# Staging eleven weight units ahead of a mixture layer, and moving its first groups' steps, in a four-layer kernel

## The chip, the cores and the metric

One NeuronCore of a Trainium2 chip. The metric is the device time of one execution of the whole program in microseconds (us); less is better. TensorE is PE in the rows (its weight loads are PEld), VectorE is DVE, ScalarE is ACT, GpSimd is POOL, and SyncE's queue, which issues most transfers, is SP.

## What is computed

2,048 tokens (16 sequences of 128) of width 256, in float32. Four residual layers follow one another:

```python
x = x + xattn0(ctx, ctx, layernorm(x))      # long convolution of key-value products
x = x + ffn0(layernorm(x))                  # 16 experts, top 4 in 2 of 4 groups, plus a shared expert
x = x + xattn1(layernorm(x), ctx, ctx)      # q.T k softmaxed over features, times v
x = x + ffn1(layernorm(x))                  # below
```

The last layer is the one that the change is about:

```python
probs = softmax(x @ Wg.T); rw, sel = top_k(probs, 2); rw = rw / rw.sum(-1)
base1, base3 = x @ W1.T, x @ W3.T           # W1, W3: (896, 256)
for k in range(2):
    x1 = base1 + lora1[sel[k]](x)           # A1: (8, 32, 256), B1: (8, 896, 32)
    x3 = base3 + lora3[sel[k]](x)
    x2 = silu(x1) * x3
    out += (x2 @ W2.T + lora2[sel[k]](x2)) * rw[k]
```

## The kernel before

The program has three blocks after one another: the first layer (to about 122 us of the span), the second layer (`moe_phase`, to about 299 us), and `tail_phase`, which does the third and the fourth layer together (299 to 789 us). Every engine's order is written by hand, as Python loops; an engine takes its instructions in that order and waits on semaphores.

**The routed loop of the second layer** (174 to 285 us) goes through 40 pairs of 128-row tiles. GpSimd gathers the rows of a tile by an indirect DMA (L1033) into a ring of eight tiles; TensorE turns them (L857), multiplies them with the expert's weights (L873, L896); ScalarE copies the result to `y_out` (L973), and SP stores it, 256 KB for a pair, into `slots_scratch` (L769). In front of the stores of pairs 0 to 3 SP issues one load of 384 KB each (L768): units 0 to 3 of the last layer's weights, into `lora_stage_early`.

**The last layer's weights** are eight chunks of 128 x 1536, cut into 16 units of 128 x 768. Units 0 and 1 are the chunk with A1, A3 and B2, units 2n+2 and 2n+3 are chunk n of the 896 hidden features. A float32 product is made of three products of a high and a low part, so each unit is split: ScalarE rounds it to `lora_w_hi` (`high_weights`, L1618), VectorE takes the difference to `lora_w_lo` (`low_weights`, L1819). The ring has four slots: unit k is loaded when unit k - 4 has been split.

**Groups and steps.** `tail_phase` takes the 16 token tiles in eight groups of two. Steps S run from -7 to 59; g = S // 7, n = S % 7. Step S of 0 to 55 is chunk n of group g. At the same time group G = g + 1 goes through the third layer and the router: `scores` at n = 0, `exponentials` and `attention_out` at n = 1, `turn` at n = 2, `logits` at n = 3, the ratio's exponential at n = 4, `spread_picks` at n = 5, `picks_copies` and `low_rank_in` at n = 6. So steps -7 to -1 are group 0's own attention, with no chunks beside them.

**A chunk's chain.** TensorE makes `base(F)` (L1442, x with W1 and W3), adds the low-rank part of the first pick `low_rank(F, 0)`, and one step later of the second, `low_rank(F, 1)` (both L1457). Behind each ScalarE makes the silu (L1625) and VectorE the product (L1953). GpSimd then weights the second pick (L1748, `weight`) and adds both (L1753, `both`), ScalarE rounds the two (L1631, L1635, `hidden_high`), VectorE makes the low parts (L1959, `hidden_low`), and two steps after `base` TensorE makes `down` and `terms` (L1489, L1502). `base(F)` waits until the products of chunk F - 2 are done, and in group 0 until chunk n is split:

```python
if g == 0:
    pe.wait_ge(lo_split, 2 * (n + 2))
if F >= 2:
    pe.wait_ge(prod_done, 2 * (F - 1))
```

The inputs of `low_rank` are the router's masks times the product with A1 and A3: `picks_copies` (ScalarE, L1678, L1682), `inputs_product` (VectorE, L1942), `inputs_high` (ScalarE, L1642, `am_hi`), and the low parts `am_lo` on GpSimd (L1759) and VectorE (L1948). GpSimd also gathers the second layer's rows of later token tiles (`gathers`, L1728), which VectorE adds to x (`add_routed`, L1829 to L1844). Group 0's wait for GpSimd's reciprocal root (L1768) stands before `normalize` (L1852). `find_inverse` and `scale_context` (L1862, L1870) make what `attention_out` (L1538) needs beside the exponentials (L1657). ScalarE's exp and silu lie in different tables, and an `ACT_TABLE_LOAD` stands where it changes; `warm` (L1684) is a one-column exponential that loads the first.

## Time and profile before

| | before |
|---|---|
| median of 3 runs | 794.3 us (794.25 to 794.47) |
| profiled execution, its own time | 791.16 us |
| its span | 789.4 us |
| TensorE busy | 713.2 us (90%), 4849 matmuls |
| VectorE busy | 507.8 us (64%) |
| GpSimd busy | 384.9 us (49%) |
| ScalarE busy | 340.5 us (43%) |
| mean granted TensorE clock | 0.959 |

The span is counted from the first instruction to the last, and the profiled execution's own time is 1.8 us more than it. A row of the timeline gives the start, the duration, the engine, the line, what is written and read and how often, and in brackets how long the engine had been idle before it and what released it.

### The profile page before, as it was taken

The numbers are of one execution on the slowest core, as the hardware profiler recorded it, in microseconds if no ns is written. First come the engines' busy times: TensorE is split into PE (matmuls) and PEld (weight loads), VectorE is DVE, ScalarE is ACT, GpSimd is POOL, SyncE is SP. The second block draws the span as 40 slices with busy tenths as digits, with TensorE's granted clock in tenths as the row PEclk, the third lists the DMA queues.
The fourth block names the chain that finished last, engine by engine and source line by source line (L and its number), as shares of the span: only waits on it lengthen the run. The fifth ranks groups of instructions, "written<-read, shape, count | busy, mean of one in ns | idle before, by whom it ended". The sixth has DMA issues, their size and how long they took to land.

```text
span 789.4 us, 13948 instructions
## 1 busy us (share of the span) xinstructions
PE 713.2 (90%) x4849; PEld 635.7 (81%) x4849; DVE 507.8 (64%) x1296; ACT 340.5 (43%) x698; POOL 384.9 (49%) x450
## 2 busy tenths in 40 slices
PE   4899988959999991778999999999999999999995
PEld 2444557848999980668899999999999999999995
DVE  3999997975666645676566566575574675653422
ACT  2563633245666652265444253444434533443221
POOL 5876956047766605544264363543652643322322
PEclk9999998988999995679999999999999999999999
DMA  8675505946866764424021020010020110000000
GB/s 246 196 166 133 142 27 125 210 108 179 245 195 197 163 146 126 155 71 130 1 61 34 8 61 28 14 59 22 29 63 5 41 41 1 2 15 1 14 1 14
DMA packets 44595, 68.61 MB, mean 87 GB/s; under 512 B 7376, under 2 KB 32240, under 8 KB 44528
## 3 DMA queue, kind: packets, MB, share of 16 engines
q0 software_dynamic: 10080, 28.72, 16.5%
q1 hardware_dynamic: 34352, 38.97, 15.5%
q8 instruction: 41, 0.67, 0.4%
q14 instruction: 26, 0.21, 0.1%
q10 hardware_dynamic: 96, 0.04, 0.0%
HBM read 50.77 MB, written 14.84 MB: 83 GB/s over the span
## 4 chain that ended last, share of the span: by engine, by line
PE 53%; POOL 3%; DVE 2%; ACT 2%; issue 2%; POOLq 0%; DVEq 0%
PE psum L1457 20%; PE psum L1442 10%; PE psum L1489 9%; PE psum L1502 4%; PE psum L1475 3%; PE psum L1538 2%; PE psum L1515 2%; PE psum L1528 2%; POOL rows_back L1728 1%; PE psum L1556 1%; ACT lora_w_hi L1618 1%; DVE lora_w_lo L1819 0%; PE psum L1546 0%; PE psum L1569 0%; PE psum L1576 0%
## 5 line engine op out<-in xcount | busy, mean ns | idle before, releaser
L1953 DVE TENSOR_TENSOR hid<-hid,psum 128x256 f32<-128x256 f32 x112 | 47.0, 420 | 152.2 <-ACT hid L1625 152.2
L1457 PE MATMUL psum<-am_hi,lora_w_hi 128*128 128x256 f32 x448 | 127.4, 284 | 2.0 <-DVE am_lo L1948 2.0
L1748 POOL TENSOR_TENSOR hid<-hid,ratio_sb 128x256 f32<-128x256 f32 x56 | 41.5, 741 | 176.9 <-DVE hid L1953 176.7
L1457 PE MATMUL psum<-am_hi,lora_w_lo 128*128 128x256 f32 x448 | 127.4, 284 | 0.0
L1457 PE MATMUL psum<-am_lo,lora_w_hi 128*128 128x256 f32 x448 | 127.2, 284 | 0.0
L1625 ACT ACTIVATE hid<-psum 128x256 f32<-128x256 f32 x112 | 42.9, 384 | 183.3 <-PE psum L1457 183.2
L1033 POOL DMA_INDIRECT rows_in<-y_scratch,slot_token x80 | 76.0, 950 | 30.9 <-issue 26.5
L1457 PEld LDWEIGHTS psum<-am_hi,lora_w_hi 128*128 128x128 f32 x448 | 86.2, 192 | 2.2 <-POOL am_lo L1759 2.1
L1457 PEld LDWEIGHTS psum<-am_hi,lora_w_lo 128*128 128x128 f32 x448 | 86.3, 193 | 0.0
L1457 PEld LDWEIGHTS psum<-am_lo,lora_w_hi 128*128 128x128 f32 x448 | 86.2, 192 | 0.0
L1728 POOL DMA_INDIRECT rows_back<-slots_scratch,comb_idx x64 | 66.8, 1043 | 39.2 <-POOLq L697 23.7
L1442 PE MATMUL psum<-lora_x_hi,lora_w_hi 128*128 128x256 f32 x224 | 67.8, 302 | 3.5 <-DVE lora_w_lo L1819 3.5
L1959 DVE TENSOR_TENSOR hid_lo<-hid,hid_hi 128x256 fp32r<-128x256 f32 x112 | 56.8, 528 | 13.1 <-ACT hid_hi L1631 8.0
L1442 PE MATMUL psum<-lora_x_lo,lora_w_hi 128*128 128x256 f32 x224 | 63.1, 282 | 0.0
L327 POOL TENSOR_TENSOR kv<-ctx_t 128x1024 f32<-128x1024 f32 (+2 forms) x48 | 57.4, 1284 | 11.6 <-PE psum L448 11.6
L1442 PE MATMUL psum<-lora_x_hi,lora_w_lo 128*128 128x256 f32 x224 | 62.9, 281 | 0.0
L873 PE MATMUL psum<-moe_w_hi,moe_xt_hi 128*128 x160 | 49.2, 307 | 0.0
L591 DVE TENSOR_TENSOR prod<-psum,q_t 128x1024 f32<-128x1024 f32 (+1 forms) x64 | 41.2, 685 | 8.4 <-PE psum L448 6.2
L1442 PEld LDWEIGHTS psum<-lora_x_hi,lora_w_hi 128*128 128x128 f32 x224 | 42.7, 191 | 4.6 <-DVE lora_w_lo L1819 4.2
L873 PE MATMUL psum<-moe_w_lo,moe_xt_hi 128*128 x160 | 45.9, 287 | 0.0
L1489 PE MATMUL psum<-hid_hi,lora_w_hi 128*128 128x512 f32 x112 | 44.6, 398 | 1.3 <-DVE hid_lo L1959 1.3
L873 PE MATMUL psum<-moe_w_hi,moe_xt_lo 128*128 x160 | 45.4, 284 | 0.0
(250 smaller groups left out, 2050.2 us busy)
## 6 DMA issues: line engine op xcount, KB each, us to landing
slots_scratch<-y_out SPq DMA_DIRECT2D x40, 256.0 KB, 3.3
stage<-in_moe_weights SPq DMA_DIRECT2D x18, 384.0 KB, 3.8
moe_w_lo<-in_moe_weights POOLq DMA_DIRECT2D x18, 384.0 KB, 7.1
lora_stage_early<-in_lora_weights SPq DMA_DIRECT2D x16, 384.0 KB, 3.5
x_sb<-in_x SPq DMA_DIRECT2D x4, 512.0 KB, 6.3
ctx_t<-in_ctx_t SPq DMA_DIRECT2D x4, 512.0 KB, 7.3
y_scratch<-y SPq DMA_DIRECT2D x8, 256.0 KB, 2.2
x_sb<-shared_out POOLq DMA_DIRECT2D x4, 512.0 KB, 5.3
```

Source lines behind the costliest of these rows:

```text
L327: last = nc.gpsimd.tensor_tensor(kv[:, n % KV_SLOTS, :, first:first + shape[2] * shape[3]].rearrange("p n (i j) -> p n i j", j=shape[3]), ...
L591: last = nc.vector.tensor_tensor(prod[:, :, j, i], y_ji, query[:, :, i].unsqueeze(2).broadcast_to(shape), ALU.mult)
L873: last = nc.tensor.matmul(gu_banks[q % 2][:, k * DIM:(k + 1) * DIM], xp, wp, start=(c == 0 and j == 0), stop=(c == HALVES - 1 and j == 2))
L1033: nc.gpsimd.indirect_dma_start(out=rows_in[:, i % ROW_SLOTS, :], out_offset=None, in_=y_dram[:, :], in_offset=bass.IndirectOffsetOnAxis(ap ...
L1442: nc.tensor.matmul(x_banks[F % 2][:, w * GT:(w + 1) * GT], wp, xp, start=(w == 0 and c == 0 and k == 0), stop=False, skip_group_check=True)
L1457: last = nc.tensor.matmul(x_banks[F % 2][:, w * GT:(w + 1) * GT], wp, ap, start=False, stop=(half == 1 and k == 2), skip_group_check=True)
L1489: last = nc.tensor.matmul(term_banks[half][:, :], wp, hp, start=(n == 0 and j == 0), stop=(n == FB - 1 and j == 2))
L1625: nc.scalar.activation(f[:, F % 2, k, :], x_banks[F % 2][:, 0:GT], ACT.Silu).then_inc(silu_done, 1)
L1728: nc.gpsimd.indirect_dma_start(out=rows_back[:, t % ROW_TILES, k * DIM:(k + 1) * DIM], out_offset=None, in_=slots_dram[:, :], in_offset=ba ...
L1748: nc.gpsimd.tensor_tensor(f[:, F % 2, 1, :], f[:, F % 2, 1, :], ratio_sb[:, F // FB % 2, :], ALU.mult)\
L1953: nc.vector.tensor_tensor(f[:, F % 2, k, :], f[:, F % 2, k, :], x_banks[F % 2][:, GT:2 * GT], ALU.mult)\
L1959: nc.vector.tensor_tensor(hid_lo[:, F % 2, which, :], f[:, F % 2, which, :], hid_hi[:, F % 2, which, :].bitcast(FP32), ALU.subtract).then_ ...
```

## The change

Eleven units instead of four are loaded in the routed loop (one in front of each of the stores of pairs 0 to 10), into three places: five slots where four were, four in `lora_stage_hidden` and two in `lora_stage_terms`. ScalarE splits all eleven at the start of `tail_phase`, ahead of its warm exponential. VectorE splits five first, two while it waits for group 0's first reciprocal root, one while it waits for the second exponential, one each in steps -6 and -5 as before, and then one a step from 0 to 5 (before: 1, 2, 2, 2, 2, 1). Units 11 to 14 are loaded early in `tail_phase`, unit 15 at step -4. Group 0's `spread_picks` stands ahead of `base(0)`. Group 1's `attention_out`, `turn`, `logits`, `router_input`, `router_top` and their counterparts on ScalarE, VectorE and GpSimd move a step on; its `exponentials` go to the end of step 1, and its `router_masks` behind `hidden_low` of step 5. A warm silu of one column stands behind group 0's `picks_copies`. At n = 0 GpSimd's gathers stand behind its other work. `hid`, `hid_hi` and `hid_lo` are allocated at another address, with no change of shape.

The core of the diff:

```diff
-                if q < STAGE_SLOTS:
-                    sp.dma_start(lora_stage[:, q, :], lora_unit(a, q)).then_inc(lora_staged, 16)
+                if q < EARLY_UNITS:
+                    sp.dma_start(unit_place(stage, q), lora_unit(a, q)).then_inc(lora_staged, 16)
...
-EARLY_UNITS = STAGE_SLOTS
+HIDDEN_SLOTS, TERMS_SLOTS = 4, 2
+HIDDEN_FIRST = STAGE_SLOTS + 1
+TERMS_FIRST = HIDDEN_FIRST + HIDDEN_SLOTS
+EARLY_UNITS = TERMS_FIRST + TERMS_SLOTS
...
+def high_units(S):
+
+    return {-6: (11, 12), -5: (13, 14), 1: (15,)}.get(S, ())
 
 
 def low_units(S):
 
-    return {-6: (4,), -5: (5,), 0: (6,), 1: (7, 8), 2: (9, 10), 3: (11, 12), 4: (13, 14), 5: (15,)}.get(S, ())
+    return {-6: (8,), -5: (9,), 0: (10,), 1: (11,), 2: (12,), 3: (13,), 4: (14,), 5: (15,)}.get(S, ())
+
+
+def late(G):
+
+    return 1 if G == 1 else 0
...
-                    if n == 1:
+                    if n == 1 + late(G):
                         attention_out(G)
-                    if n == 2:
+                    if n == 2 + late(G):
                         turn(G)
-                    if n == 3:
+                    if n == 3 + late(G):
                         logits(G)
                     if n == 3 and G == 0:
                         low_rank_in(0)
-                        base(0)
                     if n == 5:
                         spread_picks(G)
                     if n == 5 and G == 0:
+                        base(0)
                         base(1)
...
+            for k in range(EARLY_UNITS):
+                high_weights(k)
             nc.scalar.activation(warm[:, :], minus_half[:, 0:1], ACT.Exp)
-            for k in range(STAGE_SLOTS):
-                high_weights(k)
...
-                    if n == 1:
+                    if n == 1 and not late(G):
                         exponentials(G)
...
                     if n == 6:
                         picks_copies(G)
+                    if n == 6 and G == 0:
+                        nc.scalar.activation(warm[:, :], minus_half[:, 0:1], ACT.Silu)
...
                 if is_chunk(S - 1):
                     hidden_high(S - 1)
-                for k in low_units(S):
+                if n == 1 and G is not None and late(G):
+                    exponentials(G)
+                for k in high_units(S):
                     high_weights(k)
...
-                gathers(S)
+                if n > 0:
+                    gathers(S)
                 if is_chunk(S - 1):
                     weight(S - 1)
                     both(S - 1)
                 if n == 0 and 0 <= g < NG:
                     inputs_low(g, 2)
+                if n == 0:
+                    gathers(S)
...
-            for k in range(EARLY_UNITS):
+            for k in range(HIDDEN_FIRST):
                 low_weights(k)
             add_routed(0)
+            for k in range(HIDDEN_FIRST, HIDDEN_FIRST + 2):
+                low_weights(k)
             normalize(0)
...
             find_top(1)
+            low_weights(HIDDEN_FIRST + 2)
             find_inverse(1)
...
-                if n == 5 and G is not None:
+                if n == 5 and G is not None and not late(G):
                     router_masks(G)
...
                 if is_chunk(S - 1):
                     hidden_low(S - 1)
+                if n == 5 and G is not None and late(G):
+                    router_masks(G)
```

ScalarE from group 0's last copy at step -1 to the silu of chunk 0's second pick, first as it was (`hid` is the silu's output, `am_hi` an input of `low_rank`, `att_weights` the exponentials):

```order
L1682 COPY ratio_sb<-psum 128x256 [waits ratio_spread]
L1642 CAST am_hi<-mix 128x512 [waits am_mul] x3
L1625 ACT_TABLE_LOAD
L1625 ACTIVATE hid<-psum 128x256 [waits first_done]
L1642 CAST am_hi<-mix 128x512 [waits am_mul]
L1618 CAST lora_w_hi<-lora_stage_early 128x768 [waits lora_staged2]
L1657 ACT_TABLE_LOAD [waits att_done]
L1657 ACTIVATE att_weights,att_total<-psum,att_minus_top 128x256 [waits top_done]
...
L1625 ACT_TABLE_LOAD
L1625 ACTIVATE hid<-psum 128x256 [waits second_done]
```

and as it is now:

```order
L1722 COPY ratio_sb<-psum 128x256 [waits ratio_spread]
L1744 ACT_TABLE_LOAD
L1744 ACTIVATE exp_warm<-minus_half 128x1
L1682 CAST am_hi<-mix 128x512 [waits am_mul] x3
...
L1665 ACTIVATE hid<-psum 128x256 [waits second_done]
L1665 ACTIVATE hid<-psum 128x256 [waits first_done]
L1671 CAST hid_hi<-hid 128x256 [waits weighted]
L1675 CAST hid_hi<-hid 128x256 [waits both_done]
L1697 ACT_TABLE_LOAD [waits att_done]
L1697 ACTIVATE att_weights,att_total<-psum,att_minus_top 128x256 [waits top_done]
...
L1658 CAST lora_w_hi<-lora_stage_terms 128x768 [waits lora_staged15]
```

A table load and a one-column silu now stand ahead of the three `am_hi`, and the exponentials, which stood ahead of chunk 0's second silu, stand behind it and behind both `hid_hi`.

GpSimd at steps 0 and 1, before and now:

```order
L1759 TENSOR_TENSOR am_lo<-mix,am_hi 128x512 [waits am_hi_done]
L1728 DMA rows_back<-slots_scratch,comb_idx 128x256 [waits added]
L1728 DMA rows_back<-slots_scratch,comb_idx 128x256
L1759 TENSOR_TENSOR am_lo<-mix,am_hi 128x512 [waits am_hi_done]
```

```order
L1803 TENSOR_TENSOR am_lo<-mix,am_hi 128x512 [waits am_hi_done] x2
L1772 DMA rows_back<-slots_scratch,comb_idx 128x256 [waits added]
L1772 DMA rows_back<-slots_scratch,comb_idx 128x256 x3
L1772 DMA rows_back<-slots_scratch,comb_idx 128x256 [waits added]
```

The two gathers that stood between the two `am_lo` stand behind them, in a row of five with step 1's three.

VectorE from step 4's last splits to step 5's (`hid_lo` is `hidden_low`), before and now:

```order
L1959 TENSOR_TENSOR hid_lo<-hid,hid_hi 128x256 [waits hi_done] x2
L1819 TENSOR_TENSOR lora_w_lo<-lora_stage_early,lora_w_hi 128x768 [waits lora_hi_split] x2
L1926 CAST picked_masks<-lora_hit 128x512 [waits masks_spread]
L1926 CAST picked_masks<-lora_hit 128x512
L1930 TENSOR_SCALAR lora_first_sum<-lora_ratio 128x2 [waits ratio_ready]
L1931 RECIPROCAL lora_first_w<-lora_first_sum 128x2 [waits step]
L1953 TENSOR_TENSOR hid<-hid,psum 128x256 [waits silu_done] x2
L1819 TENSOR_TENSOR lora_w_lo<-lora_stage_early,lora_w_hi 128x768 [waits lora_hi_split]
```

```order
L2000 TENSOR_TENSOR hid<-hid,psum 128x256 [waits silu_done]
L2006 TENSOR_TENSOR hid_lo<-hid,hid_hi 128x256 [waits hi_done] x2
L1973 CAST picked_masks<-lora_hit 128x512 [waits masks_spread]
L1973 CAST picked_masks<-lora_hit 128x512
L1977 TENSOR_SCALAR lora_first_sum<-lora_ratio 128x2 [waits ratio_ready]
L1978 RECIPROCAL lora_first_w<-lora_first_sum 128x2 [waits step]
L1866 TENSOR_TENSOR lora_w_lo<-lora_stage_terms,lora_w_hi 128x768 [waits lora_hi_split]
```

The masks stood ahead of step 5's products and now stand between `hidden_low` and the split of unit 15.

## Rows read from the trace of the kernel before

**Rows 1.** Stretch view, TensorE: start:end, length, busy (count), clock, DMA share, GB/s
```profile
345.00:356.00 11.00, 7.45 (x33) 0.69 0.42 118
```

**Rows 2.** Waits of TensorE, 299 to 400 us: total, times, longest
```profile
PE psum L1538 <- DVE att_scaled L1870: 4.6, 2, 3.5
...
PE psum L1442 <- DVE lora_w_lo L1819: 3.5, 4, 1.3
PE psum L1457 <- DVE am_lo L1948: 2.0, 1, 2.0
```

**Rows 3.** The same from 400 us to the end
```profile
PE psum L1515 <- DVE t_lo L1975: 3.5, 1, 3.5
```

**Rows 4.** Timeline of TensorE: start, duration, line, out<-in, count, idle before
```profile
350.16 3.75 PE L1538 MATMUL psum<-att_weights,att_scaled 128*128 128x256 f32 x8 [3.55 <-DVE att_scaled L1870]
...
379.13 0.39 PE L1442 MATMUL psum<-lora_x_hi,lora_w_hi 128*128 128x256 f32 x1 [1.25 <-DVE lora_w_lo L1819]
...
385.64 0.62 PE L1569 MATMUL psum<-ident,picked_masks 128*128 128x128 bf16 x8
...
386.98 0.39 PE L1442 MATMUL psum<-lora_x_hi,lora_w_hi 128*128 128x256 f32 x1 [0.22 <-DVE lora_w_lo L1819]
```

**Rows 5.** Timeline of ScalarE
```profile
299.16 1.28 ACT L1684 ACT_TABLE_LOAD   x1 [3.79 <-PEq L697]
...
300.56 3.01 ACT L1618 CAST lora_w_hi<-lora_stage_early 128x768 fp32r<-128x768 f32 x4
...
334.71 1.07 ACT L1678 CAST masks_sb<-psum 128x512 bf16<-128x512 f32 x2 [5.51 <-PE psum L1569]
...
336.13 1.21 ACT L1642 CAST am_hi<-mix 128x512 fp32r<-128x512 f32 x2
...
339.27 0.62 ACT L1642 CAST am_hi<-mix 128x512 fp32r<-128x512 f32 x1 [1.93 <-DVE mix L1942]
...
343.24 1.28 ACT L1657 ACT_TABLE_LOAD   x1
...
346.80 1.28 ACT L1625 ACT_TABLE_LOAD   x1
...
350.63 0.40 ACT L1635 CAST hid_hi<-hid 128x256 fp32r<-128x256 f32 x1 [0.45 <-POOL hid L1753]
```

**Rows 6.** Timeline of GpSimd at steps 0 and 1
```profile
338.25 1.27 POOL L1728 DMA_INDIRECT rows_back<-slots_scratch,comb_idx  x1 [0.15 <-issue]
...
340.80 1.28 POOL L1759 TENSOR_TENSOR am_lo<-mix,am_hi 128x512 fp32r<-128x512 f32 x1
...
343.50 1.54 POOL L1728 DMA_INDIRECT rows_back<-slots_scratch,comb_idx  x1 [0.30 <-issue]
345.34 0.95 POOL L1728 DMA_INDIRECT rows_back<-slots_scratch,comb_idx  x1 [0.30 <-issue]
349.01 0.72 POOL L1748 TENSOR_TENSOR hid<-hid,ratio_sb 128x256 f32<-128x256 f32 x1 [2.73 <-DVE hid L1953]
```

**Rows 7.** Timeline of VectorE
```profile
310.78 0.41 DVE L1852 TENSOR_SCALAR att_y<-x_sb,meanvar,rstd 128x256 f32<-128x256 f32 x1 [2.63 <-POOL rstd L1768]
...
343.25 0.96 DVE L1819 TENSOR_TENSOR lora_w_lo<-lora_stage_early,lora_w_hi 128x768 fp32r<-128x768 f32 x1
...
379.86 0.75 DVE L1926 CAST picked_masks<-lora_hit 128x512 bf16<-128x512 f32 x2
...
380.72 0.17 DVE L1931 RECIPROCAL lora_first_w<-lora_first_sum 128x2 f32<-128x2 f32 x1
...
385.23 0.42 DVE L1959 TENSOR_TENSOR hid_lo<-hid,hid_hi 128x256 fp32r<-128x256 f32 x1 [0.19 <-ACT hid_hi L1635]
```

**Rows 8.** The routed loop: TensorE's wait for a gather, and two stretches
```profile
193.76 0.66 PE L857 MATMUL psum<-ident,rows_in 128*128 128x128 f32 x4 [1.95 <-DMA rows_in<-y_scratch,slot_token]
...
189.00:192.00 3.00, 2.81 (x25) 1.00 1.00 306
...
221.00:224.00 3.00, 3.00 (x28) 1.00 0.62 195
```

69 lines of the change are left out of this document (45 added, 24 removed).

## The prediction, made before the changed kernel ran

> **What bounds the kernel now.** I read the waits of TensorE first, then the stretches with the granted clock, then the timelines of TensorE, ScalarE, GpSimd and VectorE one beside the other between 299 and 390 us. Before that come the routed loop's rows. What the reader is to see is that TensorE carries the end. From 400 us on it waits for nothing but its own low parts in the last steps [rows 3], and nothing there is touched. So a microsecond that TensorE gains or loses before 390 us goes straight to the end, and work of other engines after that is free. Before 400 us the waits of TensorE in the last layer are three groups [rows 2]: 3.5 us in four waits for a split of weights, 3.55 us for group 1's attention, 2.0 us for the first `low_rank` input. After the attention wait the clock is low: the stretch 345 to 356 has a mean of 0.69 [rows 1], that is a part at 1.2 GHz and the rest at 2.4, and what runs at the lower level takes twice as long.
>
> **The splits of weights.** The last of the four waits, 0.22 us, stands before `base(6)` [rows 4] and is counted with step 5 below; the three before `base(3)` to `base(5)` are 3.5 - 0.2 = 3.3 us [rows 2]. Before, VectorE made two splits in each of steps 1 to 4, after `hidden_low`, and the second was needed by the very next `base`. Now `base(3)` needs units that were split by step -5, `base(4)` unit 11 of step 1, `base(5)` unit 13 of step 3. All are ready a step or more ahead. Late next would be the products of the chunk before last, and those show no wait at steps 6 and after. **-3.3 us.** VectorE and ScalarE do the same sixteen splits in all.
>
> **Group 1's attention.** The wait of 3.55 us ends when VectorE has scaled the context [rows 4]. Behind it stood chunk 0's second silu, delayed to 348.1 by exponentials and two table loads. Now TensorE has a whole step in front of the attention. It came to it at 350.16 - 3.55 = 346.6; step 5's products from `base` to `down` took 385.64 - 379.13 = 6.5 us [rows 4] at full clock, so it comes to it at 353.1. They can run: silu and product of chunk 0 are ready at about 346, as no exponential stands before them now.
>
> But the chain to the attention is longer too. ScalarE's exponentials now stand behind both `hid_hi` of chunk 0, and these wait for GpSimd, which has five gathers in a row ahead of `weight(0)`. Step by step:
>
> - The second GpSimd `am_lo` can start when its high part is there, 339.27 + 0.62 = 339.9 [rows 5], and ends at 341.2 (1.28 us, [rows 6]). The five gathers and that `am_lo` took from 338.25 to 349.01 - 2.73 = 346.3, so the gathers alone 6.75 us [rows 6]. They end at 348.0.
> - From `weight(0)` to the end of the second `hid_hi`: 351.03 - 349.01 = 2.0 us [rows 5, 6], to 350.1.
> - From exp's table load to the silu's load, 346.80 - 343.24 = 3.6 us [rows 5], to 353.7. Then unit 15's rounding, a quarter of 3.01 us [rows 5], to 354.4.
> - From the silu's load over chunk 1's silu, VectorE's product, reciprocals and the first scaling to the attention's start, 350.16 - 346.80 = 3.4 us [rows 4, 5], to 357.8. This is the point: VectorE's scaling stands behind the product of chunk 1, which waits for a silu behind the exponentials.
>
> The new wait is 357.8 - 353.1 = 4.7 us in place of 3.55: **+1.1 us**. Bounds: two of the gathers took 1.27 and 1.54 where a plain one takes 0.95 (that is their excess, 0.9 us); without it and without 0.3 us that the exponentials waited inside the 3.6, the wait is 3.5 and the cost 0. If two more gathers are as slow as the slowest, it is +2.3. The half-speed stretch after it stays: it now falls on `base(3)` in place of `base(2)`.
>
> **Step 5.** `hidden_low` of chunk 4 ended at 385.65; the masks and the two reciprocal steps take 380.89 - 379.86 = 1.0 us and stood before the step's products, hidden behind waits. Now they stand between it and unit 15's split (0.96 us, [rows 7]), and `base(6)` waits for that split: 385.65 + 1.0 + 1.0 = 387.65 where it started at 386.98 [rows 4]. **+0.7 us**, bounds 0.3 (if TensorE's own picks end later anyway) and 1.0.
>
> **Picks ahead of `base(0)`, and the warm silu.** 6.5 us for a step of 54 units of 256 columns (42 short matmuls, six double ones) is 0.12 each, so `base(0)` is 12 of them, 1.4 us: ScalarE's copies of the picks start at 333.3 in place of 334.71 [rows 5]. The first `am_hi` came 1.42 us behind them, so it would be at 334.7. But a table load and a one-column silu stand between now; the same pair at the start of the block took 300.56 - 299.16 = 1.4 us up to the next copy [rows 5]. So `am_hi` starts at 336.1, where it was, and the wait of 2.0 us stays. The table load that goes away at step 0 was hidden behind TensorE's `low_rank`. **0 us.** The Trainium skill (ScalarE: Activation LUTs, What ACT_TABLE_LOAD costs) gives 1.28 us for the load plus a drain of 1.38 at each switch; by it the inputs would come 1.4 us later than before and the sum would be 1.4 us worse. The load's 1.28 agrees with the trace, the drain doesn't show in it: the copy follows load and warm exponential within 0.1 us.
>
> **The block's start.** ScalarE rounds eleven units from 299.2 without waiting for its table, VectorE five, and both are done before the first gathered rows. Units 5 and 6 (1.9 us) go into VectorE's wait of 2.63 us for the reciprocal root [rows 7], unit 7 into a later one of about its length. The risk is GpSimd: a gather beside a split took 1.54 us in place of 0.95 [rows 6, 7]. Two gathers stand beside units 5 and 6, ahead of that root, which TensorE's first scores wait for. Bounds 0 and 1.2 us, and a gain of 0.4 if the earlier start lets a gather be issued undisturbed; most gathers beside VectorE's work are not slowed. **+0.3 us.**
>
> **The routed loop.** Seven more loads of 384 KB go out, one with each pair, 2.8 us apart (40 pairs in 111 us). A plain stretch moves 195 GB/s, a load in each pair adds 141, together 336; with loads the loop reached 306 at a DMA share of 1.00 [rows 8]. 30 GB/s too much over seven pairs is 0.6 MB, or 1.9 us of backlog at most. TensorE waited 1.95 us for a gather right there [rows 8], once, and never after, as GpSimd issues a tile in 1.25 us and so gets 0.3 us further ahead with each pair. Bounds 0 and 1.9. **+0.3 us**, near the lower bound, since the lead has grown when the backlog is largest. The Trainium skill (DMA: Bandwidth & Descriptors, Queues, rings and completion order) says that each DMA engine takes turns between queues packet by packet; by it the gathers' own queue would be shielded from SP's and the cost 0. The trace agrees only in part: the wait of 1.95 us fell among those loads.
>
> **Sum.** -3.3 + 1.1 + 0.7 + 0 + 0.3 + 0.3 = -0.9 us. For the profiled execution that is 791.2 - 0.9 = 790.3; the median of the runs is 3.1 us above it, and 794.3 - 0.9 gives **793.4 us**. A measurement tells some 0.2%, 1.6 us, from no change; the forecast is inside that.
>
> **The rivals.**
>
> 1. **The attention's chain is as short as its bounds allow.** Gathers at 0.95, the wait 3.5 as before, step 5 at 0.3, nothing lost before: -3.3 + 0.3 = -3.0, 791.3 us. For it: most gathers are at 0.95. Against it: those in question run beside VectorE's split and reductions, where the two slow ones were. Chance 0.24.
> 2. **The warm silu is free.** If its load were done while ScalarE waits for the picks, `am_hi` would come 1.4 us earlier, the wait of 2.0 would shrink to 0.6, and the clock would probably stay up, saving 1.3 us on twelve matmuls at half speed: 790.7. Against it: it stands behind the ratio's copy in ScalarE's order. Chance 0.10.
> 3. **The loads starve the gathers (slower).** In the routed loop, between 200 and 222 us, TensorE's turn of a pair waits for rows as at 193.76. Two more such waits, 3.9 us, in place of my 0.3: -1.2 + 3.9 = +2.7, 797.0. It decides the sign from a backlog on that delays gathers by more than their lead. Against it: no wait after 194 us though loads went on until 201 and the share stayed high. Chance 0.17.
> 4. The upper ends of attention, step 5 and start together: -3.3 + 2.3 + 1.0 + 1.2 = +1.2 to +3 with the loop: chance 0.05 of over 1.6.
> 5. **The wait for attention vanishes**, as the move a step on intends if the exponentials were early: -3.3 - 3.55 + 1.3 = -5.5, 788.8. Their place behind `hid_hi` speaks against it; chance 0.02.
>
> The forecast has 0.42. So faster 0.36 (rivals 1, 2 and 5), within 0.2% 0.42, slower 0.22 (3 and 4). The range reaches to rivals 1 and 2 below and nearly to rival 3 above: 790.5 to 796.8; the forecast's own is 792.7 to 795.0.
>
> **What the changed profile should show.** No wait of TensorE for `lora_w_lo` before `base(3)` to `base(5)`, one of up to a microsecond before `base(6)`. A wait of 4 to 5 us before the attention matmuls, now behind `down(0)`, ended by the scaling, and at half clock after it. The first `am_hi` at 37 us after the block's start, as before, and the wait before `low_rank(0, 0)` near 2 us. `weight(0)` right behind five gathers in a row, at about 348 us. Splits of units 5 and 6 within VectorE's wait for the root. DMA share near 1.00 from 203 to 222 us with TensorE busy throughout. I would be wrong if the routed loop ends more than a microsecond later, or if the attention's wait is under 3 or over 6 us.

## The result, and the profile after

The change takes the kernel from 794.3 us (median of four runs, 793.1 to 794.5) to **788.9 us** (four runs, 788.7 to 790.3): a ratio of 0.9942, interval [0.9927, 0.9957], or 5.4 us. The forecast was 793.4, with a range that ended at 790.5. It is wrong by 4.5 us, to the fast side.

The two profiled executions differ by less: spans of 789.4 and 787.0 us. The one of before took 791.16 us where the median is 794.3, the one of the change 788.73 where the median is 788.9. So the two traces alone can't account for all of it, and what follows rests on more than one profile of each.

TensorE's waits in the changed kernel, 299 to 401 us (total, times, longest), answer to [rows 2]:

```profile
PE psum L1578 <- DVE att_scaled L1917: 5.0, 2, 4.0
...
PE psum L1497 <- DVE am_lo L1995: 1.9, 1, 1.9
...
PE psum L1609 <- DVE picked_masks L1973: 0.3, 1, 0.3
PE psum L1482 <- DVE lora_w_lo L1866: 0.2, 1, 0.2
```

The three waits for a split are gone and the 0.2 us ahead of `base(6)` stays. The longest wait, for the attention, grew from 3.55 to 4.0 us. TensorE's timeline answers to [rows 4], with the stretch around the attention behind it (start:end, length, busy time and count of TensorE, its weight loads, VectorE, ScalarE and GpSimd, then clock, DMA share, GB/s):

```profile
360.07 3.75 PE L1578 MATMUL psum<-att_weights,att_scaled 128*128 128x256 f32 x8 [4.00 <-DVE att_scaled L1917]
...
387.33 0.39 PE L1482 MATMUL psum<-lora_x_hi,lora_w_hi 128*128 128x256 f32 x1 [0.23 <-DVE lora_w_lo L1866]
...
356.00:368.00 12.00, 8.00 (x37) 7.25 (x37) 8.13 (x23) 3.68 (x7) 3.49 (x4) 0.72 0.17 45
```

ScalarE (answers to [rows 5]): the warm Silu's load and activation, the first `am_hi`, the exponentials' load behind the second `hid_hi`, chunk 1's silu load.

```profile
337.80 1.28 ACT L1744 ACT_TABLE_LOAD   x1
339.09 0.20 ACT L1744 ACTIVATE exp_warm<-minus_half 128x1 f32<-128x1 f32 x1
339.20 1.12 ACT L1682 CAST am_hi<-mix 128x512 fp32r<-128x512 f32 x2
...
352.32 0.41 ACT L1675 CAST hid_hi<-hid 128x256 fp32r<-128x256 f32 x1 [0.41 <-POOL hid L1797]
352.75 1.28 ACT L1697 ACT_TABLE_LOAD   x1
...
356.71 1.28 ACT L1665 ACT_TABLE_LOAD   x1
```

The block's start on GpSimd and VectorE, and then GpSimd's gathers ahead of `weight(0)` (answers to [rows 6, 7]):

```profile
301.81 1.63 POOL L1772 DMA_INDIRECT rows_back<-slots_scratch,comb_idx  x1 [0.30 <-issue]
303.75 1.44 POOL L1772 DMA_INDIRECT rows_back<-slots_scratch,comb_idx  x1 [0.30 <-issue]
...
310.64 1.51 POOL L1772 DMA_INDIRECT rows_back<-slots_scratch,comb_idx  x1 [0.30 <-issue]
...
344.46 1.01 POOL L1772 DMA_INDIRECT rows_back<-slots_scratch,comb_idx  x1 [0.15 <-issue]
...
349.76 0.94 POOL L1772 DMA_INDIRECT rows_back<-slots_scratch,comb_idx  x1 [0.30 <-issue]
350.72 0.75 POOL L1792 TENSOR_TENSOR hid<-hid,ratio_sb 128x256 f32<-128x256 f32 x1
```

```profile
300.80 4.43 DVE L1866 TENSOR_TENSOR lora_w_lo<-lora_stage_early,lora_w_hi 128x768 fp32r<-128x768 f32 x5 [0.61 <-ACT lora_w_hi L1658]
306.92 1.34 DVE L1876 TENSOR_TENSOR x_sb<-x_sb,rows_back 128x256 f32<-128x256 f32 x3 [1.69 <-DMA rows_back<-slots_scratch,comb_idx]
...
309.51 1.82 DVE L1866 TENSOR_TENSOR lora_w_lo<-lora_stage_hidden,lora_w_hi 128x768 fp32r<-128x768 f32 x2
312.85 0.41 DVE L1899 TENSOR_SCALAR att_y<-x_sb,meanvar,rstd 128x256 f32<-128x256 f32 x1 [1.52 <-POOL rstd L1812]
```

**A ledger.** Total times scatter by 2 to 3 us from one execution to the next. The last layer's block alone repeats to some tenths, so I measure there. The marks are starts in the timelines: the block (VectorE's cast of `ident`), the first `att_y`, the first copy of `lora_x_t`, the first `am_hi`, the first `low_rank` matmul, and the ratio copies R1, R2 and R7 of groups 1, 2 and 7; the end is that of VectorE's last instruction. The columns are the pieces between marks in us; the change ran three times (two of them in runs told of below).

| kernel | block to att_y | to x_t | to am_hi | to low_rank | to R1 | to R2 | to R7 | to end | sum |
|---|---|---|---|---|---|---|---|---|---|
| before | 11.58 | 14.77 | 10.58 | 2.66 | 48.25 | 55.48 | 274.67 | 69.75 | 487.7 |
| before, repeated | 11.56 | 14.77 | 10.70 | 2.66 | 48.32 | 55.48 | 274.65 | 69.75 | 487.9 |
| changed | 12.89 | 15.75 | 10.60 | 2.64 | 45.42 | 55.22 | 273.19 | 68.84 | 484.6 |
| changed, repeated | 12.96 | 14.81 | 10.89 | 2.64 | 44.23 | 55.22 | 273.24 | 69.64 | 483.6 |
| changed, loads later | 12.93 | 15.75 | 10.60 | 2.64 | 45.45 | 55.27 | 273.19 | 68.91 | 484.7 |

So the block is 3.0 to 4.3 us shorter. The piece from the first low-rank matmul to R1, which holds all the steps that the change moves, is 2.8 to 4.1 us shorter where the forecast's terms for it come to -1.5 (-3.3 + 1.1 + 0.7). And the groups 2 to 7, whose work the forecast took as untouched, give 1.7 us (0.26 + 1.45). These are the two things to explain. The piece up to `x_t` takes 14.8 or 15.7 us, whichever kernel it is: the mean clock in it is 0.62 where it is short and 0.50, all of it at 1.2 GHz, where it is long.

### The profile page after: what moved, and what is told of

Read it like the earlier page. It is cut to its first block, busy times and chain, and to the rows that moved or that the text cites. A ratio compares the mean times of both kernels' runs of the same rounds, so it can differ in the third digit from the quotient of the medians.

```text
span 787.0 us, 13949 instructions
## 1 busy us (share of the span) xinstructions
PE 711.4 (90%) x4849; PEld 635.8 (81%) x4849; DVE 508.9 (65%) x1296; ACT 340.7 (43%) x699; POOL 385.8 (49%) x450
## 4 chain that ended last, share of the span: by engine, by line
PE 53%; POOL 3%; issue 2%; ACT 2%; DVE 2%; POOLq 0%; DVEq 0%; ACTq 0%
PE psum L1497 19%; PE psum L1482 10%; PE psum L1529 9%; PE psum L1542 5%; PE psum L1515 3%; PE psum L1578 2%; POOL rows_back L1772 2%; PE psum L1568 2%; PE psum L1555 1%; PE psum L1596 1%; PE psum L1586 1%; PE psum L1609 0%; PE psum L1616 0%; ACT att_weights L1697 0%; POOL am_lo L1803 0%
## 5 line engine op out<-in xcount | busy, mean ns | idle before, releaser
L1772 POOL DMA_INDIRECT rows_back<-slots_scratch,comb_idx x64 | 64.8, 1012 | 38.8 <-POOLq L704 22.4
L2006 DVE TENSOR_TENSOR hid_lo<-hid,hid_hi 128x256 fp32r<-128x256 f32 x112 | 58.4, 537 | 14.6 <-ACT hid_hi L1671 8.5
L327 POOL TENSOR_TENSOR kv<-ctx_t 128x1024 f32<-128x1024 f32 (+2 forms) x48 | 57.3, 1283 | 11.6 <-PE psum L448 11.6
L1797 POOL TENSOR_TENSOR hid<-hid 128x256 f32<-128x256 f32 x56 | 43.4, 774 | 4.4
```

The costliest lines, as they stand in the source:

```text
L327: last = nc.gpsimd.tensor_tensor(kv[:, n % KV_SLOTS, :, first:first + shape[2] * shape[3]].rearrange("p n (i j) -> p n i j", j=shape[3]), ...
L1772: nc.gpsimd.indirect_dma_start(out=rows_back[:, t % ROW_TILES, k * DIM:(k + 1) * DIM], out_offset=None, in_=slots_dram[:, :], in_offset=ba ...
L1797: nc.gpsimd.tensor_tensor(f[:, F % 2, 0, :], f[:, F % 2, 0, :], f[:, F % 2, 1, :], ALU.add)\
L2006: nc.vector.tensor_tensor(hid_lo[:, F % 2, which, :], f[:, F % 2, which, :], hid_hi[:, F % 2, which, :].bitcast(FP32), ALU.subtract).then_ ...
```

## The experiments

Theory at the start: my terms with their sizes off, the staging above all. Rival: what came better lies in work that I took as untouched. In the tables the last column is the ratio to the kernel before on the same chip; "R1" is the piece from the first `low_rank` matmul to R1.

**The change again, and three parts undone.** The first run is the change unedited. The edits of the others:

no_late:

```
-    return 1 if G == 1 else 0
+    return 0
```

gathers_back:

```
-                if n > 0:
-                    gathers(S)
+                gathers(S)
...
-                if n == 0:
-                    gathers(S)
```

no_warm:

```
-                    if n == 6 and G == 0:
-                        nc.scalar.activation(warm[:, :], minus_half[:, 0:1], ACT.Silu)
```

> The changed kernel itself once more, to see how far single executions and profiles of either kernel scatter. If the difference of the medians (5.4 us) is the change's own, it comes back within 1 us, 4.5 to 6.5 us below the kernel before. If the kernel before merely ran at a slow moment (its profiled execution was 3.1 us under its median), the difference is 2 to 4 us.

> The changed kernel with group 1's attention, turn, logits and masks back at their old steps (late always 0). My theory from the two traces: the move a step on costs 0.45 us at the attention's wait and 0.57 us at step 5, so without it the time is about 1 us less than the changed kernel's. Rival: the move is what made the gain, by giving TensorE a step of work behind the exponentials; then the time is 2 us or more above the changed kernel's.

> The changed kernel with GpSimd's gathers at n = 0 ahead of its other work again. From 387 us on the changed kernel gained 0.3 us with each group: VectorE's t_lo took 0.95 us in place of 1.19, as GpSimd's addition no longer ran beside it. If the place of the gathers does that, this kernel is 1.5 to 2.5 us slower than the changed one, and its t_lo takes 1.19 us again. Rival: another address of hid, or the phase that the start of the layer leaves the engines in, does it; then it is within 0.7 us of the changed kernel and t_lo stays at 0.95.

> The changed kernel without the one-column silu behind group 0's picks. If its table load holds up the first inputs, they come 1.4 us earlier, TensorE's wait of 1.9 us before the first low-rank product falls to 0.5, and the time is 1.4 us less (2.5 if the clock then stays at 2.4 GHz over it). Rival: the load was only moved, and the silu's own load at step 0 falls on TensorE's path in its place; then the time is the same or up to 1.3 us more.

| run | x_t to am_hi | R1 | attention wait | R2 to R7 | ratio, interval |
|---|---|---|---|---|---|
| again | 10.89 | 44.23 | 2.94 | 273.24 | 0.9932 [0.9909, 0.9955] |
| no_late | 10.99 | 42.51 | 2.86 | 273.20 | 0.9906 [0.9874, 0.9938] |
| gathers_back | 10.98 | 42.86 | 2.47 | 273.20 | 0.9936 [0.9912, 0.9959] |
| no_warm | 9.58 | 44.52 | 4.38 | 273.19 | 0.9914 [0.9887, 0.9940] |

The repetition's 0.9932 is 5.6 us, so the 5.4 us of the medians are the change's own and no slow moment of the kernel before.

Group 1's late attention costs 1.7 us against the repetition and 2.9 against the first profile, so its sign was right (+1.8 forecast with step 5). In total no_late is 2.1 us below the repetition (1 expected), with intervals that overlap. Part of that cost is the gathers' new place: undone, it gives back 1.4 to 2.6 us (1.0 to 2.2 in a second run, told of below), since two of the five gathers are then issued ahead of a low part and no longer stand in one block in front of `weight(0)`. The warm Silu is not free: without it `am_hi` is 1.0 to 1.3 us earlier, near the 1.4 that I had expected, and the wait ahead of `low_rank` falls from 1.9 to 0.6 us. Part of the gain is kept: from `x_t` to R1 no_warm needs 56.8 us, the repetition 57.8 and the first profile 58.7. TensorE comes to the attention 1.6 to 2.7 us earlier, counted from `x_t`, but the chain it waits for ends only 1.2 us earlier, so this wait is now 4.4 us, the longest of all. The total, 0.9914 beside 0.9932, does not tell the two apart.

```profile
PE psum L1578 <- DVE att_scaled L1915: 5.4, 2, 4.4
...
PE psum L1497 <- DVE am_lo L1993: 0.6, 1, 0.6
```

All four have 273.2 us from R2 to R7, so neither the late step nor the Silu is needed for that gain, and by this one run the gathers' place isn't either (a second run, below, says more). In gathers_back `t_lo` took 0.69 us, neither the 1.19 nor the 0.95 that were expected.

**The place of `hid`, later splits, earlier exponentials, later loads.** The only other thing of the change that I know to reach the groups 2 to 7 is that `hid`, `hid_hi` and `hid_lo` are allocated elsewhere. hid_only makes this edit in the kernel before; the other three edit the change.

hid_only:

```
     y, scaled, z = (sb(n, [P, TG, DIM]) for n in ("att_y", "att_scaled", "lora_y"))
+    f = sb("hid", [P, 2, PICKS, GT])
+    hid_hi, hid_lo = (sb(n, [P, 2, 2, GT], F32R) for n in ("hid_hi", "hid_lo"))
...
-    f = sb("hid", [P, 2, PICKS, GT])
-    hid_hi, hid_lo = (sb(n, [P, 2, 2, GT], F32R) for n in ("hid_hi", "hid_lo"))
```

splits_later (`low_units`, and VectorE's list at the block's start):

```
-    return {-6: (8,), -5: (9,), 0: (10,), 1: (11,), 2: (12,), 3: (13,), 4: (14,), 5: (15,)}.get(S, ())
+    return {-6: (5,), -5: (6,), -4: (7,), -3: (8,), -1: (9,), 0: (10,), 1: (11,), 2: (12,), 3: (13,), 4: (14,), 5: (15,)}.get(S, ())
...
-            for k in range(HIDDEN_FIRST, HIDDEN_FIRST + 2):
-                low_weights(k)
...
-            low_weights(HIDDEN_FIRST + 2)
```

exps_first:

```
+                if n == 1 and G is not None and late(G):
+                    exponentials(G)
                 if is_chunk(S - 1):
                     hidden_high(S - 1)
-                if n == 1 and G is not None and late(G):
-                    exponentials(G)
```

loads_later:

```
-                if q < EARLY_UNITS:
-                    sp.dma_start(unit_place(stage, q), lora_unit(a, q)).then_inc(lora_staged, 16)
+                if 12 <= q < 12 + EARLY_UNITS:
+                    sp.dma_start(unit_place(stage, q - 12), lora_unit(a, q - 12)).then_inc(lora_staged, 16)
```

> The kernel before with one edit: hid, hid_hi and hid_lo are allocated right behind lora_y, as in the change, and nothing else of the change. From the ratio copy of group 2 to that of group 7 the profile of before has 274.67 us, and the changed kernel and all four of its variants 273.19 to 273.24, though their code for these groups is the one of before. Theory A (where hid lies in SBUF sets what VectorE's and GpSimd's reads and writes cost each other, above all t_lo at 1.19 against 0.94 and 0.69 us): 273.2 +- 0.15 here, and 1.5 to 1.8 us less in all than before. Theory B (the two have settled on different orders of arrival at low_rank_out, set by what happens ahead of group 2, and the address has no part): 274.7 here, no change in the time. Theory C (chance of one execution): anywhere between.

> The changed kernel with VectorE's differences of units 5, 6 and 7 taken out of the start of the block (two stood between add_routed(0) and normalize(0), one between find_top(1) and find_inverse(1)) and put into the steps -6 to -4, the later ones a step on. Theory A (VectorE's longer list ahead of the steps, and GpSimd's gathers that lengthen beside it from 0.95 to 1.5 us, cost what was found between the block's start and the first att_y, 12.9 against 11.6 us, and all of it stays): the first att_y 1.0 to 1.3 us earlier from the block's start (11.6 to 11.9), the first copy of lora_x_t at 26.9 to 27.6 in place of 27.8 to 28.7, the total 0.5 to 1 us less. Theory B (the splits only move and are paid at steps -6 to -4, where ScalarE and VectorE already hold up the first group): att_y earlier, but the first am_hi at the same 38.7 to 39.7 us.

> The changed kernel with one edit on ScalarE: in group 1's step 1 the exponentials stand ahead of hidden_high of chunk 0 in place of behind it. Theory A (TensorE's wait of 2.9 to 4.0 us ahead of group 1's attention is for the end of a chain that begins with these exponentials, so it shrinks by the time of hidden_high and its wait for VectorE's product): the wait falls by 1.5 to 3 us, the ratio copy of group 1 comes 1 to 2.5 us earlier after the first low-rank matmul (44.2 in the repeated run, 45.4 in the first). Theory B (hidden_high is what TensorE's down projection or low_rank_out of chunk 0 then waits for; the wait changes its place): the wait at attention shrinks and another one of the same size comes up ahead of the down matmuls of chunk 0, the ratio copy at the same place within 0.5 us.

> The changed kernel with its 11 weight loads issued at pairs 12 to 22 of the routed loop in place of 0 to 10, where the load of DMA is at its height (share 1.00, 306 GB/s at 189 to 192 us, against 0.62 and 195 GB/s at 221 to 224). Theory A (the 11 loads of 393 KB lengthen the stretch of the routed loop that is bound by DMA, worth 0.8 to 2 us of it): the block starts 1 to 2 us earlier than in the repeated run of the change on the same chip. Theory B (all that a load takes from the gathers at the start comes back before the loop's end): the block starts at the same time within 0.5 us. Against either stands that this chip's loop itself scatters from one execution to another.

| run | block to att_y | R1 | attention wait | R2 to R7 | block to end | ratio, interval |
|---|---|---|---|---|---|---|
| hid_only | 11.50 | 48.27 | 3.46 | 273.20 | 485.6 | 0.9952 [0.9927, 0.9976] |
| splits_later | 12.42 | 45.71 | 4.33 | 273.24 | 484.1 | 0.9952 [0.9932, 0.9972] |
| exps_first | 12.92 | 41.43 | 1.20 | 273.24 | 479.4 | 0.9895 [0.9866, 0.9924] |
| loads_later | 12.93 | 45.45 | 4.01 | 273.19 | 484.7 | 0.9919 [0.9890, 0.9948] |

**exps_first** is the clearest. With ScalarE's exponentials ahead of `hidden_high(0)` the attention wait falls to 1.2 us, and the stretch at half speed behind it is gone. The stretch 356 to 368 of this run had 0.72 in the change at the same place:

```profile
356.00:368.00 12.00, 10.02 (x67) 8.93 (x65) 10.65 (x28) 3.19 (x8) 5.52 (x7) 1.00 0.22 61
```

So R1 is 2.8 us shorter than in the change's repetition and 4.0 shorter than in its first profile, more than the 1 to 2.5 of theory A. Of this 1.6 and 2.6 us are matmul time (38.38 us busy, against 39.95 and 40.93), at 2.4 in place of 1.2 GHz. The rest, 1.2 and 1.4, is idle time: the wait gave 1.7 and 2.8, but others took some of it back, 0.5 us ahead of `down`, which is what theory B named, and 0.8 us ahead of the turn of `lora_y` (0.3 in the repetition).

**splits_later** missed: `att_y` came at 12.42, not 11.6 to 11.9. Its gathers still show 1.63 and 1.44 us. These two lie beside the first five splits, which VectorE begins at once, since ScalarE's rounding no longer waits for a table load; only the last gather's 1.51 was due to the splits that I moved. And what it gained at the start was lost again at the attention. **loads_later** is inconclusive: its last `y_out` copy is at 294.8 us, that of the change at 296.6, but splits_later, whose routed loop is the change's, has 294.8 too, exps_first 297.5 and hid_only, without the seven more loads, 296.6. The loop's own scatter covers the price of 0 to 1.9 us.

**hid_only** gives the whole 1.5 us of the groups 2 to 7 with nothing else of the change, and nothing in the R1 piece. By theory A this is the address. But is it?

**The kernel before again, the staging alone, and two faster versions.** staging_only is the change with late attention, gathers, Silu and the picks' order all undone: the first three edits above and the one shown here. exps_cold is exps_first without the Silu activation; exps_cold_split has splits_later's edit as well.

```
                         low_rank_in(0)
+                        base(0)
...
                     if n == 5 and G == 0:
-                        base(0)
                         base(1)
```

> The kernel before, unedited, to see what of its profile belongs to the kernel and what to one execution. Theory A (with hid at its old address VectorE and GpSimd meet at low_rank_out so that t_lo takes 1.2 us, in every execution): 274.7 us from the ratio copy of group 2 to that of group 7 and t_lo at 1.19 to 1.21 again, where the kernel with hid moved alone had 273.20 and 0.69. Theory B (a chance of the one profiled execution): 273.2 here. Of the rest: the first ratio copy of group 1 lies 87.84 us after the block's start in the first profile; the changed kernel's repetitions scatter by 2 us there (85.2 to 87.4), through the stretches at half clock, so 86 to 90 is expected.

> The changed kernel with four of its parts undone: group 1's attention at its old steps, GpSimd's gathers at their old place, no Silu activation ahead of the steps, base(0) behind low_rank_in(0) again. What is left is the staging of 11 units with its splits, and the place of hid. Theory A (the three waits of 3.5, 3.5 and 2.0 us less what stays of them, put at 3.3 us of idle, is the gain, with some 0.2 us a stall on top): from the first low-rank matmul to the ratio copy of group 1 48.25 us before and 48.27 with hid moved alone; 44.6 to 45.0 here, and the first am_hi as late after the first lora_x_t as before (10.6). Theory B (a stall costs its idle and also a stretch at half clock behind it, so that fewer stalls are worth more): 42 to 43.5 here. The version without the late attention, but with the picks ahead and the Silu, had 42.51. In all 4 to 6 us below the kernel before by B, 3 to 4 by A.

> The changed kernel with the exponentials ahead of hidden_high(0) in group 1's step 1, as in the run before, and without the Silu activation at step -1. The first of these alone took the wait ahead of attention down to 1.20 us and kept the clock at full speed behind it (54.80 us from the first lora_x_t to the ratio copy of group 1, where the changed kernel had 57.76 and 58.66); the second alone brought the first am_hi 1.3 us forward and gave it back at attention (wait 4.38, 56.79 us). Theory A (they add, since the chain that the second waited for is the one that the first shortens): 53.0 to 53.8 us, 0.8 to 1.8 us less than the first alone in all. Theory B (attention's chain becomes the bound again, on VectorE): the wait grows to 2.5 us or more, 54.5 us and more, no gain in all.

> The kernel of the run ahead of it, with the three splits taken out of the start of the block as well (units 5 to 7 at steps -6 to -4). Alone that brought the first lora_x_t to 27.20 us from the block's start (27.7 to 28.7 in the other variants) and the first am_hi to 37.62 (38.5 to 39.7), and lost a part of it at attention, with a wait of 4.33 us. Theory A (it adds here, with attention's chain shortened): the ratio copy of group 1 0.7 to 1.2 us earlier from the block's start than without it. Theory B (VectorE's list in steps -6 to -3 is then what holds the masks and the products back): the same time within 0.4 us, or later.

| run | x_t to am_hi | R1 | attention wait | R2 to R7 | ratio, interval |
|---|---|---|---|---|---|
| before_again | 10.70 | 48.32 | 3.45 | 274.65 | 0.9980 [0.9952, 1.0007] |
| staging_only | 10.89 | 42.63 | 3.15 | 274.46 | 0.9913 [0.9878, 0.9948] |
| exps_cold | 9.33 | 40.80 | 1.21 | 273.76 | 0.9869 [0.9831, 0.9906] |
| exps_cold_split | 10.09 | 40.83 | 1.20 | 273.80 | 0.9905 [0.9875, 0.9935] |

The repetition of before has 274.65 us from R2 to R7: theory A, and not a chance of one execution. The staging alone takes **5.7 us** out of the R1 piece (48.3 to 42.6), not 3.3. (The place of `hid`, which it has too, is worth nothing here: 48.27 in hid_only.) That is theory B's number; whether it is theory B's reason, the stretch view tells, from the first low-rank matmul to R1 (columns as above). First before, then staging_only:

```profile
338.79:387.04 48.25, 41.18 (x269) 38.07 (x269) 31.74 (x79) 26.98 (x52) 19.16 (x21) 0.89 0.28 83
```
```profile
372.03:414.66 42.63, 39.48 (x271) 37.13 (x272) 28.65 (x75) 20.64 (x42) 18.39 (x21) 0.92 0.14 38
```

Idle time falls by 3.9 us (48.25 - 41.18 = 7.1 to 42.63 - 39.48 = 3.2): the four split waits of 3.5 and 0.4 of the attention's. TensorE's busy time falls by 1.7 us for the same matmuls, with the clock up from 0.89 to 0.92. But these 1.7 us do not lie behind the waits for splits. The stretches between changes of the clock, two of before and then the one of staging_only around its attention:

```profile
349.16:355.99 6.83, 5.83 (x19) 5.15 (x20) 6.29 (x15) 2.28 (x4) 1.42 (x3) 0.50 0.34 93
355.99:387.04 31.05, 27.53 (x208) 25.64 (x206) 19.78 (x52) 16.02 (x31) 11.20 (x13) 1.00 0.24 74
```
```profile
382.76:386.18 3.42, 3.15 (x8) 2.56 (x9) 2.85 (x7) 1.42 (x3) 0.70 (x1) 0.50 0.52 151
```

In before the waits for splits, of 0.2 to 1.3 us, all fall into the second stretch, 31.05 us with 3.5 idle, and the clock stays at 1.00 through it. What shrank is the stretch at 1.2 GHz around the attention, from 6.8 to 3.4 us; the one behind the first `low_rank` wait is 3.4 us in both. The forecast had no term for that. The attention's wait is 3.15 us in staging_only, 3.55 in before. Over all eighteen profiles the clock was low for 6.8 us around the attention where this wait was 3.45 to 4.4 us (both runs of before, hid_only twice, the change's first profile, loads_later, splits_later, no_warm), for 3.4 us where it was 2.5 to 3.15, and not at all where it was 1.2. The length of a wait alone doesn't decide it: gathers_only, below, has 3.4 us at 1.2 GHz behind a wait of 1.28 us for a split, and before has none behind one of 1.31.

The picks ahead of `base(0)` are worth nothing beside the Silu: no_late, which has both, needs 42.51.

exps_cold brings both of the edits together: the waits ahead of `low_rank` (0.6) and attention (1.2) are short, the clock is 1.00 over the whole piece, and `am_hi` is 1.4 us earlier than in exps_first. Up to R1, counted from the block's start, it is 2.0 us ahead of exps_first and 7.3 us ahead of before (52.8 us from `x_t` to R1, where theory A had 53.0 to 53.8):

```profile
PE psum L1578 <- DVE att_scaled L1915: 2.2, 2, 1.2
...
PE psum L1497 <- DVE am_lo L1993: 0.6, 1, 0.6
```

By R7 exps_cold has given back 0.7 of the 2.0 us that it is ahead of exps_first; the other 1.3 go in the last piece, where its last `low_rank_out` ran at half speed and that of exps_first did not. Over the block the two need 479.3 and 479.4 us. The splits moved in addition make it 1.6 us later at R1, 0.3 of which lies ahead of `x_t`, and 0.9 of the clock at the first scores is in that (theory B, with the clock's part by chance): the wait ahead of `low_rank` is 1.7 us again.

And staging_only, where `hid` has its new place too, has 274.46 us from R2 to R7, with `t_lo` at 1.27. The address alone can't be the whole answer.

**What sets the groups 2 to 7.**

gathers_only makes this edit in the kernel before; the other three runs repeat kernels of above.

```
-                gathers(S)
+                if n > 0:
+                    gathers(S)
...
+                if n == 0:
+                    gathers(S)
```

> The kernel before with one edit of the change alone: at a group's first step GpSimd issues its gathers behind weight, both and inputs_low(g, 2) in place of ahead of them. Theory A (the edit takes both of chunk 3 off t_lo: in the change both begins 0.46 us behind t_lo, t_lo takes 0.94, and low_rank_out does not wait): t_lo 0.94 +- 0.03 and 273.2 us from the ratio copy of group 2 to that of group 7, 1.5 to 1.8 us less in all than the kernel before. Theory B (the place of hid or the start of the block does it, not this edit): t_lo 1.20 and 274.7. Theory C (a tie that falls one way or the other): 0.69 or 1.2 to 1.3.

> A second time the kernel before with hid's place alone moved, which had t_lo at 0.69 and 273.20 us. Theory A (the place sets it): the same again. Theory B (t_lo and both start together, and which of the two is served first is settled anew in each execution or on each chip): 0.69 and 273.2, or 1.2 to 1.3 and 274.5 to 274.7; a value of the second kind here refutes A.

> A second time the change with the gathers at their old place, which had t_lo at 0.69 and 273.20 us, with both beginning 0.01 us ahead of it. Theory A (fixed by the program): the same. Theory B (a tie, settled anew): either 0.69 and 273.2, or 1.27 and 274.5.

> A second time the staging alone, which had t_lo at 1.27 and 274.46 us though its code and its addresses in these groups are those of the run above. Theory A (fixed by the program, through what comes ahead of group 2): the same. Theory B (a tie, settled anew): either kind. Besides, the piece from the first low-rank matmul to group 1's ratio copy took 42.63 us, and no part of either theory touches it: 42.5 to 42.8 again, where TensorE's clock does not differ.

| run | t_lo at step 2 of groups 1 to 5 | R1 to R2 | R2 to R7 | gathers at | hid at |
|---|---|---|---|---|---|
| before, twice | 1.19 to 1.22 | 55.48 | 274.66 | old | old |
| hid_only, twice | 0.68 to 0.69 | 55.16 | 273.20 | old | new |
| gathers_only | 0.85 to 0.88 | 55.26 | 273.83 | new | old |
| changed and repetitions | 0.93 to 0.96 | 55.2 to 55.3 | 273.2 | new | new |
| exps_cold, exps_cold_split | 1.02 to 1.11 | 55.4 | 273.8 | new | new |
| gathers_back | 0.69 | 55.28 | 273.20 | old | new |
| gathers_back_2 | 1.25, 1.27, 0.68, 1.27, 1.27 | 55.56 | 274.17 | old | new |
| staging_only | 1.27 | 55.03 | 274.46 | old | new |
| staging_only_2 | 0.68, 1.27, 0.68, 1.27, 1.27 | 54.77 | 274.18 | old | new |

(In total gathers_only had a ratio of 0.9979 [0.9957, 1.0002]; the three repetitions ran once each. The R1 piece of staging_only_2 is 42.57 us, that of gathers_back_2 43.27.) The first of the five `t_lo` lies between R1 and R2, the other four between R2 and R7, and each long one costs 0.3 us: none gives 273.20, three give 274.17 and 274.18, four give 274.46. gathers_only fits none of its theories, hid_only_2 fits both of its own, and gathers_back_2 and staging_only_2 are as theory B had it. The timelines of VectorE, GpSimd and TensorE around the `low_rank_out` of group 5's step 2 show what goes on. Before:

```profile
637.75 1.20 DVE L1975 TENSOR_TENSOR t_lo<-mix,t_hi 128x512 fp32r<-128x512 f32 x1
...
637.65 0.74 POOL L1753 TENSOR_TENSOR hid<-hid 128x256 f32<-128x256 f32 x1
...
638.79 0.28 PE L1502 MATMUL psum<-lora_w_hi,hid_lo 128*128 128x256 f32 x1
639.00 0.38 PE L1515 MATMUL psum<-lora_w_hi,t_hi 128*128 128x256 f32 x1
...
639.34 0.28 PE L1515 MATMUL psum<-lora_w_hi,t_lo 128*128 128x256 f32 x1
```

hid_only_2, the same instructions:

```profile
661.09 0.68 DVE L1975 TENSOR_TENSOR t_lo<-mix,t_hi 128x512 fp32r<-128x512 f32 x1
...
661.09 1.29 POOL L1753 TENSOR_TENSOR hid<-hid 128x256 f32<-128x256 f32 x1
...
662.47 0.28 PE L1515 MATMUL psum<-lora_w_hi,t_lo 128*128 128x256 f32 x1
```

And the change:

```profile
636.64 0.95 DVE L2022 TENSOR_TENSOR t_lo<-mix,t_hi 128x512 fp32r<-128x512 f32 x1
...
636.28 0.75 POOL L1792 TENSOR_TENSOR hid<-hid,ratio_sb 128x256 f32<-128x256 f32 x1
637.11 1.08 POOL L1797 TENSOR_TENSOR hid<-hid 128x256 f32<-128x256 f32 x1
...
637.67 0.28 PE L1542 MATMUL psum<-lora_w_hi,hid_lo 128*128 128x256 f32 x1
637.79 0.28 PE L1555 MATMUL psum<-lora_w_hi,t_hi 128*128 128x256 f32 x1
...
638.01 0.28 PE L1555 MATMUL psum<-lora_w_hi,t_lo 128*128 128x256 f32 x1
```

`t_lo` and GpSimd's `both` meet. Where `both` begins 0.1 us ahead (before), it keeps its 0.74 us and `t_lo` takes 1.20 in place of 0.69, which TensorE's `low_rank_out` waits for: 1.6 us from the start of `t_lo` to the third matmul, against 1.4 in the others, and 0.3 us a group in all. No wait is recorded for it: the first matmul of `low_rank_out` only starts 0.21 us behind the one ahead of it, and takes 0.38, where the change has 0.12 and 0.28. Where the two begin together, one of them pays: `both` at 1.29 in hid_only_2, or `t_lo` at 1.27. Within one execution it went either way:

```profile
553.36 0.68 DVE L2019 TENSOR_TENSOR t_lo<-mix,t_hi 128x512 fp32r<-128x512 f32 x1
...
608.03 1.27 DVE L2019 TENSOR_TENSOR t_lo<-mix,t_hi 128x512 fp32r<-128x512 f32 x1
...
662.98 1.27 DVE L2019 TENSOR_TENSOR t_lo<-mix,t_hi 128x512 fp32r<-128x512 f32 x1
```

That is gathers_back_2. So neither A nor B alone: the place of `hid` takes away the 0.1 us by which `both` led (in both runs of hid_only, and in all with `hid` at its new and the gathers at their old place) and leaves a tie, which fell well in hid_only and ill in most groups of staging_only. The gathers' new place puts `both` 0.5 us behind `t_lo`, and the tie is gone; `t_lo` then meets `weight`, which began 0.36 us ahead of it (0.9 us in every group, and 273.2). In exps_cold `weight` begins only 0.22 to 0.26 us ahead, so it ends later, `t_lo` takes 1.04 to 1.08 and 0.6 us of the gain is gone. In gathers_only `t_lo` is as short as 0.85 to 0.88 and the five groups still need 0.6 us more than in hid_only; that, and why another address shifts VectorE and GpSimd by a few hundredths of a us, was not found.

## Why the prediction was wrong

The forecast was -0.9 us. In the ledger the block gained 3.0 to 4.3, and the total 5.4. Point by point, in its own order:

- **The splits of weights, -3.3 us.** The failing step, together with the last point of this list. The three waits went as described, and the splits needed by `base(3)` to `base(5)` were early enough. But staging_only puts the term at -5.7 (42.63 us, 42.57 in its second run, against 48.25): 3.5 of waits for splits, 0.2 of them counted under step 5, then 0.4 off the attention's wait, and 1.7 of matmul time, as the stretch at half speed around the attention shrank from 6.8 to 3.4 us. I had written that this stretch "stays", and so had priced the staging at three waits and nothing else. With the late attention added, it stayed in two of the change's three profiles and shrank in the third. Why the staging shortens the attention's wait by 0.4 us was not traced.
- **Group 1's attention, +1.1 us, and step 5, +0.7.** Together +1.8, measured +1.7 to +2.9 as the difference to no_late; the upper end holds 1.7 us of matmul time at half speed. The chain was right link by link: five gathers in a row (344.46 to 350.70, 6.2 us, put at 6.75), exponentials behind `hid_hi` at 352.75, then 4.0 us to the silu's load (put at 4.4 with unit 15's rounding), 3.4 to the attention (put at 3.4). The wait is 4.0 us, put at 4.7, and one repetition had 2.9, just under the 3 at which I had said I would be wrong, with half-speed matmuls behind it in all three. `base(6)` waits 0.23 us as before, but the piece from the picks to it is 1.5 us, 0.1 longer; the picks themselves now wait 0.33, as the masks are late. The rival with a vanishing wait priced the change at 788.8, and 788.9 was measured: luck, since the wait did not vanish. Yet what it named as its condition, exponentials ahead of `hid_hi`, was the best edit found.
- **Picks ahead and warm Silu, 0 us.** Right, and for the reason given: ScalarE's load at 337.80 and activation push `am_hi` to where it was (10.6 us after `x_t`, before 10.6). Without the Silu it comes 1.0 to 1.3 us earlier. Here the Trainium skill (ScalarE: Activation LUTs, What ACT_TABLE_LOAD costs) would add a drain of 1.38 us to the load's 1.28. The trace has an activation 1.29 us behind the load's start, in this place as in the others, and no drain.
- **Block's start, +0.3 us.** Measured +1.35, just above my upper end of 1.2. Three gathers were slowed in place of one. I had looked for the two beside units 5 and 6; the others stand beside the first splits, which now begin earlier. The clock at the first scores adds 0 or 1 us, by chance.
- **The routed loop, +0.3 us.** The rival of starved gathers did not happen: TensorE's waits for `rows_in` are 10.9 us in the changed profile and 9.4 in [rows 8]'s kernel, and 11.0 in hid_only, which has none of the seven more loads. From 203 to 222 us the DMA share is 0.97 and TensorE busy for 18.8 of 19.0 us, as foretold. The last `y_out` copy is 1.8 us later in the one pair of profiles, more than the microsecond at which I would call myself wrong, but within what the loop scatters by (294.8 to 297.5 us in the six kernels named). The price is not settled.
- **From 400 us on, "nothing there is touched".** Wrong. The trace of before showed no wait of TensorE's to gain there, and I took the absence of a recorded wait for the absence of a gain. Two side effects, `hid`'s address and the order of GpSimd's list, gave 1.7 us. This is the second failing step: a term put at nothing. Besides, the last twelve `low_rank_out` matmuls ran at half speed in both profiles of before and partly at full speed in two of the three of the change, up to 0.9 us more. That is chance: in both runs of hid_only, the kernel before but for an address, the last piece was shorter still (68.4 and 68.5 us).

With the measured sizes the sum is -5.7 (staging) + 1.7 to 2.9 (late attention) + 1.35 (start) + 0 to 1 (clock at the scores) - 1.7 (groups 2 to 7) - 0 to 0.9 (end), which is -5.3 to -2.2 at its ends and -3.0 to -4.3 as found in single profiles. The measured total of -5.4 is 1.1 to 2.4 us more than that. The unedited kernel before, measured against itself, came out at 0.998, 1.6 us, with an interval that holds 1, and gathers_only has 1.7 us in total where its block gives 0.3. So this remainder can't be told from the error of the comparison, and it stays open.
